# A graph network on one core: self edges taken into the last weighing steps, and messages summed before they are reduced

## The reference

```
xl, xr = x @ Wl + bl, x @ Wr + br
e = leaky_relu(xl[src] + xr[dst], 0.2)
logits = einsum('ehc,hc->eh', e, att)
p = exp(logits - segment_max(logits)[dst])
alpha = p / (segment_sum(p)[dst] + 1e-16)
out = segment_sum(xl[src] * alpha).mean(over heads) + bias
x = batchnorm(leaky_relu(out, 0.01) + x)
```

## Time and profile before

| what | value |
|---|---|
| median of 3 runs | 7120.96 us |
| the profiled execution | 7123.42 us |
| its span | 7121.3 us |
| VectorE busy | 6159.4 us, 86% |
| TensorE busy | 5928.9 us, 83% |
| GpSimd busy | 4853.9 us, 68% |
| ScalarE busy | 3368.9 us, 47% |
| mean granted clock of TensorE | 0.804 of full |

### The profile page before, as it was taken

The page is one execution under the profiler, slowest core; times in us unless marked ns, Lnnn a source line. Parts: engine busy times, 40 slices in busy tenths (PEclk is TensorE's granted clock), DMA queues, the critical chain, the costliest instruction groups (busy, mean ns, idle before and its releaser), DMA issues.

```text
span 7121.3 us, 170234 instructions
## 1 busy us (share of the span) xinstructions
PE 5928.9 (83%) x26044; PEld 4528.5 (64%) x26045; DVE 6159.4 (86%) x12236; ACT 3368.9 (47%) x10977; POOL 4853.9 (68%) x7291
## 2 busy tenths in 40 slices
PE   0589898897579889898668898888866999999998
PEld 0366666665456666666446666666555888888887
DVE  7689999897679999999668999999868999999999
ACT  0155555555135555555414555555623444444444
POOL 1788888781388878886068788887325666666665
PEclk8899999999599999999879999999965555555555
DMA  2211111111011111112011111111101111111111
GB/s 86 61 35 35 36 35 39 35 36 11 13 38 36 39 33 36 36 36 32 0 27 41 34 35 36 35 40 34 18 1 46 32 31 31 32 31 31 32 31 29
DMA packets 214545, 237.87 MB, mean 33 GB/s; under 512 B 72925, under 2 KB 195902, under 8 KB 213950
## 3 DMA queue, kind: packets, MB, share of 16 engines
q1 hardware_dynamic: 93630, 163.53, 7.7%
q0 software_dynamic: 120704, 72.40, 7.4%
HBM read 222.44 MB, written 13.20 MB: 33 GB/s over the span
## 4 chain that ended last, share of the span: by engine, by line
PE 35%; DVE 25%; issue 20%; DVEq 13%; POOL 5%; DMA 1%; POOLq 1%; ACT 0%; ACTq 0%; SPq 0%
PE psum L672 15%; PE psum L657 11%; DVE xs L1557 4%; PE psum L659 3%; DVEq L1225 3%; DVEq L1542 3%; POOL xg L502 3%; DVE acc L1569 2%; DVE u L1191 2%; PE psum L645 2%; DVE acc L1232 2%; DVEq L1021 2%; DVE u L1551 1%; DVE oht L1186 1%; PE psum L648 1%
## 5 line engine op out<-in xcount | busy, mean ns | idle before, releaser
L502 POOL DMA_INDIRECT xg<-table,idx x2808 | 2883.7, 1027 | 714.2 <-PE psum L648 252.5
L657 PE MATMUL psum<-wz,xt 128*128 x5928 | 1822.6, 401 | 49.8 <-ACT xt L922 49.7
L672 PE MATMUL psum<-px,oh 128*128 128x272 f32 x5616 | 1645.1, 417 | 258.6 <-DVE acc L1232 242.9
L672 PEld LDWEIGHTS psum<-px,oh 128*128 128x128 f32 x5616 | 961.9, 191 | 653.2 <-DVE acc L1232 437.8
L657 PEld LDWEIGHTS psum<-wz,xt 128*128 128x128 f32 x5928 | 1001.8, 197 | 408.2 <-issue 65.6
L557 POOL DMA_INDIRECT xg<-table,idx x936 | 911.7, 974 | 507.2 <-DVE xs L1557 282.3
L1191 DVE SCALAR_TENSOR_TENSOR u<-psum,atts 128x512 f32<-128x512 f32 x1482 | 1013.4, 684 | 218.8 <-PE psum L659 218.1
L803 PE MATMUL psum<-w2e,xt 65*128 65x256 f32 x1872 | 1057.0, 668 | 138.8 <-DVE xs L1557 74.1
L1199 DVE TENSOR_REDUCE lr<-u 128x16 f32<-128x512 f32 x1482 | 1012.6, 685 | 107.4 <-DVE u L1191 58.8
L1218 DVE TENSOR_TENSOR px<-xs,pg 128x528 f32 (+1 forms) x1404 | 990.3, 706 | 80.0 <-PE psum L672 39.8
L851 ACT ACTIVATE dist<-iota_f,ndloc 128x128 f32<-128x128 f32 x2808 | 974.2, 394 | 95.9 <-PE psum L672 73.3
(11 more groups left out here) (271 smaller groups left out, 7715.0 us busy)
## 6 DMA issues: line engine op xcount, KB each, us to landing
dr<-dlocs SPq DMA_DIRECT2D x468, 192.0 KB
xg<-table,idx POOLq DMA_INDIRECT x3744
at<-w_rows SPq DMA_DIRECT2D x156, 192.0 KB, 3.2
fl<-flags SPq DMA_DIRECT2D x30, 576.2 KB
flags<-fl SPq DMA_DIRECT2D x10, 576.2 KB, 3.2
table<-xn SPq DMA_DIRECT2D x3, 784.0 KB, 3.6
xp<-keys SPq DMA_DIRECT2D x5, 385.0 KB, 4.4
u<-keys SPq DMA_DIRECT2D x5, 385.0 KB, 4.5
```

Source lines behind the costliest of these rows:

```text
L502: nc.gpsimd.indirect_dma_start(out=xg[:, s % S6, t, 96:128], out_offset=None, in_=table, in_offset=bass.IndirectOffsetOnAxis(ap=idx[:, s, ...
L657: pe.matmul(out_z, xt[:, r, e * P:(e + 1) * P], wz[:, bass.ds(l, 1), :].rearrange("p o z -> p (o z)"), start=True, stop=False)
L672: last = pe.matmul(agg_ps(r), oh[:, s % 3, e, :], px[:, s % 3, e, :], start=(e == 0), stop=(e == 1))
```

## The change

**In each layer** the self loop is dissolved into the weighing tail. On every engine each three of the 36 steps take one round: on VectorE the new `last_body` does, for the three steps, weigh, add, `weighted`; weigh, add, `weighted`, `over_channels`; weigh, add, `over_channels`, two logits. On TensorE the first two steps are `aggregate` and then one `zed`, the third is `aggregate` and two `self_front`. On ScalarE `weights_of` is followed by two `self_keep`, two `self_rows` or two `linear`. Twelve of the thirteen rounds go this way, the thirteenth stands behind. The number of operations stays.

**In the equivariant part** b is no longer reduced over its inputs before the sum. TensorE sums b itself by destination: the new `sum_messages` has four matmuls of 192 columns (24 outputs x 8 of the 16 inputs, both halves accumulating into the same 8 places) and two of 32, and VectorE reduces the result, nine places for each of the 32 outputs, from PSUM (`sum_inputs`, 288 wide), and adds it to `acc1` from SBUF a step later. The reduction of b (768 wide) and the second operation of `messages` go. b gets six buffers, one for each slot, and a wait for `ag1_done` of six steps earlier. `radial` is one matmul of 384 columns for each half with all 128 partitions (the upper 63 rows are zeroed once) in place of one of 256 and one of 128 columns with 65. `prepare` is split: its first operation stands behind b of the batch's last step, its second (`scalar_product`) behind the reduction of a. The read of the block number stands ahead of a. GpSimd's part is not touched.

```diff
+
+        def sums_ps(r):
+            return psum[:, 6 + r, 0:9 * C].rearrange("p (g t) -> p g t", t=9)
...
-        mv = in_l1([2, 6, 24])
-        rp = in_l1([6, 24])
+        rp = in_l1([C])
...
-        w2e = sb("w2e", [65, 384])
-        pb = xs[:].rearrange("p a b c d -> p (a b c d)")[:, 0:4 * 384].rearrange("p (a e i x) -> p a e i x", a=2, e=2, i=3)
+        w2e = sb("w2e", [P, 384])
+        pb = xs[:].rearrange("p a b c d -> p (a b c d)")[:, 0:S6 * 768].rearrange("p (a e i x) -> p a e i x", a=S6, e=2, i=3)
...
-                pe_group(l, GROUPS, False, True, LASTB)
-
                 for r in range(2):
                     self_front(l, r, r)
-                with pe.Fori(0, SELF // 2 - 1) as i:
-                    for r in range(2):
-                        zed(l, NS + i * 2 + r, r)
-                    for r in range(2):
-                        self_front(l, i * 2 + 2 + r, r)
+                with pe.Fori(0, LASTB) as i:
+                    for s in range(S6):
+                        m = (i * 2 + s // 3) * 2
+                        aggregate(l, GROUPS - 1, ((GROUPS - 1) * BODIES + i) * S6 + s, s)
+                        if s % 3 < 2:
+                            zed(l, NS + m + s % 3, s % 3)
+                        else:
+                            for r in range(2):
+                                self_front(l, m + 2 + r, r)
                 for r in range(2):
                     zed(l, NS + SELF - 2 + r, r)
...
-                    rows = hid[0:65, r, e * P:(e + 1) * P]
-                    pe.matmul(z_ps(r, 0, HC)[:, e, :], rows, w2e[:, 0:HC], start=True, stop=True)
-                    last = pe.matmul(psum[:, 4 + r, e * P:(e + 1) * P], rows, w2e[:, HC:HC + P], start=True, stop=True)
+                    rows = hid[:, r, e * P:(e + 1) * P]
+                    last = pe.matmul(psum[:, 2 * r + e, 0:HC + P], rows, w2e[:], start=True, stop=True)
...
+                pe.wait_ge(pb_done, HELD + k + 1)
                 pe.wait_ge(ad_done, HELD + k - 1)
+                parts = sums_ps(r)
                 for e in range(2):
-                    last = pe.matmul(psum[:, 6 + r, 0:C], oh[:, r, e, :], msg[:, s // 3, 2 * (s % 3) + e, 0:C], start=(e == 0), stop=(e == 1))
+                    prod = pb[:, s, e].rearrange("p i (u t) -> p (i u) t", t=16)
+                    for h in range(2):
+                        pe.matmul(parts[:, 0:24, 0:8], oh[:, r, e, :], prod[:, :, 8 * h:8 * h + 8],
+                                  start=(e == 0 and h == 0), stop=(e == 1 and h == 1))
+                for e in range(2):
+                    last = pe.matmul(parts[:, :, 8], oh[:, r, e, :], msg[:, s // 3, 2 * (s % 3) + e, 0:C], start=(e == 0), stop=(e == 1))
                 last.then_inc(ag1_done, 1)
...
-                with act.Fori(0, SELF // 2 - 1) as i:
-                    for r in range(2):
-                        self_keep(l, i * 2 + r, r)
-                    for r in range(2):
-                        self_rows(l, i * 2 + 2 + r, r)
-                    for r in range(2):
-                        linear(l, NS + i * 2 + r, r, NS // J + i * 2 + r, r, 0)
+                with act.Fori(0, LASTB) as i:
+                    for s in range(S6):
+                        p = i * 2 + s // 3
+                        weights_of(l, GROUPS - 1, i, s)
+                        for r in range(2):
+                            if s % 3 == 0:
+                                self_keep(l, p * 2 + r, r)
+                            if s % 3 == 1:
+                                self_rows(l, p * 2 + 2 + r, r)
+                            if s % 3 == 2:
+                                linear(l, NS + p * 2 + r, r, NS // J + p * 2 + r, r, 0)
...
+            def last_body(l, i, starts):
+                k0 = ((GROUPS - 1) * BODIES + i) * S6
+                for s in range(S6):
+                    m = (i * 2 + s // 3) * 2
+                    weigh_rows(l, GROUPS - 1, i, k0 + s, s)
+                    if s > 1 or not starts:
+                        add_sums(l, GROUPS - 1, k0 + s - 2, s % 2, block_at(k0 + s - 2))
+                    if s % 3 < 2:
+                        weighted(l, NS + m + s % 3, s % 3)
+                    if s % 3 > 0:
+                        r = s % 3 - 1
+                        over_channels(l, NS + m + r, r, NS // J + m + r, r, 0)
+                    if s % 3 == 2:
+                        for r in range(2):
+                            logits(l, NS + m + r, r, 1, self_l[:, bass.ds(m * 2 + 2 * r, 2), :])
...
-                dve_group(l, GROUPS, False, True, LASTB)
-
-                with v.Fori(0, SELF // 2) as i:
-                    for r in range(2):
-                        weighted(l, NS + i * 2 + r, r)
-                    for r in range(2):
-                        over_channels(l, NS + i * 2 + r, r, NS // J + i * 2 + r, r, 0)
-                    for r in range(2):
-                        logits(l, NS + i * 2 + r, r, 1, self_l[:, bass.ds(i * 4 + 2 * r, 2), :])
-
+                last_body(l, 0, True)
+                with v.Fori(1, LASTB) as i:
+                    last_body(l, i, False)
+                for r in range(2):
+                    add_sums(l, GROUPS - 1, NS - 2 + r, r, block_at(NS - 2 + r))
+                for r in range(2):
+                    weighted(l, NS + SELF - 2 + r, r)
+                for r in range(2):
+                    over_channels(l, NS + SELF - 2 + r, r, NS // J + SELF - 2 + r, r, 0)
+                for r in range(2):
+                    logits(l, NS + SELF - 2 + r, r, 1, self_l[:, 2 * SELF - 4 + 2 * r:2 * SELF - 2 + 2 * r, :])
...
+            seq(op.memset(hid[64:128, :, :], 0.0))
             op.memset(hid[64:65, :, :], 1.0)
+            for r in range(2):
+                op.memset(psum[:, 6 + r, 0:9 * C], 0.0)
             v.wait_ge(ln_sqrt, 2)
...
-            def products(k, s, batch, adds=None):
+            def products(k, s, batch, adds=None, summed=None, following=None):
 
 
                 r, half, n = s % 2, s // 3, 2 * (s % 3)
+                b = block_of(summed) if summed is not None else None
                 v.wait_ge(rr_done, AHEAD + k + 1)
                 v.wait_ge(dt_done, HELD + batch + 1)
                 v.wait_ge(pr_done, HELD + k - 1)
...
+                if summed is not None:
+                    add_messages(summed, b)
                 v.wait_ge(q_done, HELD + batch + 1)
                 v.wait_ge(fq_done, AHEAD + batch + 1)
-                v.wait_ge(vr_done, HELD + k - 1)
+                v.wait_ge(ag1_done, AHEAD + k + 1 - S6)
                 op.tensor_tensor(
-                    pb[:, r].rearrange("p e i (u t) -> p e i u t", t=16),
-                    psum[:, 4 + r, 0:2 * P].rearrange("p (e u t) -> p e u t", e=2, t=16).unsqueeze(2).to_broadcast([P, 2, 3, 8, 16]),
+                    pb[:, s].rearrange("p e i (u t) -> p e i u t", t=16),
+                    z_ps(r, HC, HC + P).rearrange("p e (u t) -> p e u t", t=16).unsqueeze(2).to_broadcast([P, 2, 3, 8, 16]),
                     gq[:, half, n:n + 2].unsqueeze(3).to_broadcast([P, 2, 3, 8, 16]), ALU.mult).then_inc(pb_done, 1)
-                b = block_of(adds) if adds is not None else None
+                if following is not None:
+                    prepare(*following)
                 v.wait_ge(pa_done, HELD + k + 1)
...
                 op.tensor_reduce(msg[:, half, n:n + 2, 24:40], pa[:, r].rearrange("p e (u t) -> p e u t", t=16), AX.X, ALU.add).then_inc(pr_done, 1)
-                v.wait_ge(pb_done, HELD + k + 1)
-                if s % 3 == 0:
-                    v.wait_ge(msg_done, HELD + batch - 1)
-                op.tensor_reduce(mv[:, half, n:n + 2, :], pb[:, r].rearrange("p e i (u t) -> p (e i u) t", t=16), AX.X, ALU.add).then_inc(vr_done, 1)
+                if following is not None:
+                    scalar_product(*following)
                 if adds is not None:
-                    add_messages(adds, (s + 3) % S6, b)
+                    sum_inputs(adds, (s + 3) % S6)
...
-                op.tensor_tensor(along, msg[:, half, :, 32:40].unsqueeze(2).to_broadcast([P, 6, 3, 8]),
+                op.tensor_tensor(msg[:, half, :, 0:24].rearrange("p n (i u) -> p n i u", u=8),
+                                 msg[:, half, :, 32:40].unsqueeze(2).to_broadcast([P, 6, 3, 8]),
                                  unit[:, bass.ds(k, 3)].rearrange("p s e i -> p (s e) i")[:, :, 0:3].unsqueeze(3).to_broadcast([P, 6, 3, 8]),
-                                 ALU.mult).then_inc(rp_done, 1)
-                v.wait_ge(rp_done, HELD + batch + 1)
-                v.wait_ge(vr_done, HELD + k + 3)
-                op.tensor_tensor(msg[:, half, :, 0:24], rp, mv[:, half], ALU.add).then_inc(msg_done, 1)
-
-            def add_messages(k, s, b):
+                                 ALU.mult).then_inc(msg_done, 1)
...
+            def sum_inputs(k, s):
 
                 v.wait_ge(ag1_done, AHEAD + k + 1)
                 v.wait_ge(ad_done, HELD + k)
```

(22 more changed lines are left out.)

42 lines of the change are left out of this document (16 added, 26 removed).

## The result

The changed kernel takes 7211.16 us (median of 4 runs, 7184.77 to 7227.51), the kernel before 7121.58 beside it: ratio 1.0123, 95% interval [1.0111, 1.0135]. It is slower by 90 us where I had forecast 20, and lies above my range. The profiled execution is the fastest of the four: span 7182.9 us at a mean granted TensorE clock of 0.911, against 7121.3 before. The others had spans of 7200.9, 7217.8 and 7225.7 at 0.906, 0.905 and 0.899.

What follows compares the result with a forecast made beforehand. It took chains of short hand-overs to bound the layers' tails and VectorE the equivariant part, with GpSimd next. 7123.4 + 120 (tail) - 100 (equivariant part) = 7143 profiled, median 7141; 8 in 10 range 7080 to 7200.

Steps and rivals of the forecast that it cites:

- The wait in the last stage: Weighing tail: VectorE's `weighted` waits for the projection queued behind `aggregate`, 2.5 us, twice in three steps.
- Three steps in 11.6 us: Weighing tail on VectorE: three steps with a round take 11.6 us for 9.05 before, 29 us more a layer.
- the 88 of the sum: Weighing tail at the upper clock: 88 us more for three layers, part of the tail's +120.
- my bound for reads that all stand open (12.4): Weighing tail: three steps take 12.4 us if no read of the block number is hidden.
- The clock, a quarter of the time (32 us): Weighing tail: TensorE at the lower clock a quarter of the time, 10.5 us a layer, 32 for three.
- The rule against me: Weighing tail: the skill's clock falls only after idling longer than any pause here, so the tail would stay warm.
- The warm tail: Rival: the tail keeps the upper clock and GpSimd alone bounds the equivariant part, -26 us, 7095; chance 0.27.
- The equivariant part, -100: Equivariant part: upper clock, 10.2 us a batch, 104 us gained over 150 batches, less 4 added once.
- the exposed read: Rival, equivariant part: late sums expose the block number's read once a batch, 10.6 us a batch, 7202; chance 0.08.
- the cold tail (7193): Rival: the tail is at the lower clock for two thirds of the time or more, +72 us; chance 0.18.

Runs made afterwards that it cites:

- g1_pe_order: Changed kernel with only TensorE's order in the last stage turned, each projection ahead of its step's `aggregate`: 7774.24 us in one run, on the slower chips.
- e3_filler: Changed kernel with four extra unread matmuls behind each projection of the interleaved tail: 7964.36 us, ratio 1.0193 to the kernel before, on the slower chips.
- h3_before_128_rows: Kernel before with only the radial product's rows filled up with zeros from 65 to 128: 7118.73 us in one run.
- e1_equi: Kernel before with the change in the equivariant part alone: 7778.0 us, ratio 0.9949 to the kernel before, on the slower chips.
- after_again: Changed kernel as it is, run again beside the kernel before on the slower chips: 8015.55 us, ratio 1.0271.

## Why the prediction was wrong

- *The wait in the last stage*: right in kind and size. Forecast 2.5 us twice in three steps, measured 2.49; g1_pe_order shows that the place of the projection behind `aggregate` makes it.
- *Three steps in 11.6 us*: this term failed. With the clock up they take 12.3 to 12.5 us, and a layer 39.6 us more instead of 29 (e3_filler): 119 us for the 88 of the sum. That this is just my bound for reads that all stand open (12.4) is luck, for the third step's read is hidden, as I had it (add 0.62 us behind its weighing). Two things were missing. I had let the read of the second step lie beside `weighted`; it starts only behind the weighing, since VectorE's queue stands at `weighted`'s wait, and 0.27 us of it shows. And I had no idle time ahead of a three's first weighing: 0.46 us for the sum, 0.75 where the loop turns.
- *The clock, a quarter of the time (32 us)*: this term failed too, right in kind and too small. In the profiled execution it cost 55 us, and a mean of 0.80 over the three stages means the lower level for 0.4 of their time. The other runs lie 18 to 43 us above that one at clocks of 0.899 to 0.906; that this too is the clock of the last stages is inferred from the mean clock, since these have no trace. The median would then be 119 + 55 + 26 = 200 for the tail, and 200 - 110 = 90.
- *The rule against me*: by the section that the prediction names of the Trainium skill ("TensorE: Matmul & The Clock Gate"), the tail would have stayed warm. This case's trace disagrees: the clock fell though TensorE waited no longer than 2.46 us at a time, and 0.74 to 0.83 was granted over the three stages. The warm tail (7095) failed twice over, since a warm tail alone, with 119 us for 88, is no gain either: 7123.4 + 119 - 110 = 7132.
- *The equivariant part, -100*: right, -110. The clock is 1.00, the copies of indices lie 10.1 us apart in nearly all batches and 10.17 in the mean (10.2 was forecast), the exposed read did not come. h3_before_128_rows shows that TensorE was not the bound before. This holds for the faster chips; on the others the part is 20 us shorter in e1_equi's profile and 22 longer in after_again's.
- *The range*: the cold tail (7193) was the nearest case of my list, though its clock for two thirds of the time (84 us) is more than the 55 of the profiled execution; with the chain at 119 as well it is 7123.4 + 119 + 84 - 110 = 7216. I had named both ends (12.4 us, and a clock low for two thirds) but never added them up.

## What to carry to other kernels

Before interleaving two chains, write down for each engine what stands ahead of the instruction that the other engine waits for: here two swapped lines decide between +58 and -10 us a layer. Work that needs only old inputs goes ahead of work that waits for the present step. Judge a fully busy TensorE by its granted clock first: at 0.50 it was 96% busy and was not the bound. A read moved ahead wants work beside its new place, and the head of a loop's body has none. And where two costs have bounds and one cause (a chain too slow), add their far ends up, since they come together.
